# Expert loop started before the last shared sum, result rows released by the next down product, expert numbers loaded in fours, first batch's statistics at the loop's end

## The chip, the cores and the metric
One core of one Trainium2 chip runs the whole program. The metric is device time in microseconds (us) of one execution; less is better. The kernel before took 603.58 us (median of 3 runs, 598.58 to 605.2).

## The reference
Tokens are 2 batches of 1024, 128 wide, float32. Three blocks run in a row, each adding to or replacing the activations:

1. a recurrent mixing block (RWKV-like, 16 heads), its output projected,
2. a feed-forward block with 32 experts (used twice: after block 1 and after block 3),
3. a hierarchical block attention over 5 levels, 16 heads of 64.

The feed-forward block is what the change is about. In short:

```
x_n   = layernorm(x)
probs = x_n @ gate_w ; e = argmax ; score = sigmoid(max)      # one expert per token
routed = (silu(r @ gate_e) * (r @ up_e)) @ down_e,  r = x_n * score
shared = (silu(x_n @ sg) * (x_n @ su)) @ sd
x      = x + shared + routed
```

The attention block begins with a layernorm of x and a projection to queries, keys and values for 8 pairs of heads and 2 batches.

## The kernel before, in words
The program is written by hand: each engine (TensorE, VectorE, ScalarE, GpSimd, SyncE) has its own instruction list, and semaphores order them. There is no planner. The order of the lists is: mixing block (`a_*`), feed-forward 0 (`f_*`, k = 0), attention (`b_*`), feed-forward 1 (`f_*`, k = 1), stores.

**Routing.** Every token is written with its row number into a DRAM table `sorted_x` that is sorted by expert, in slots of 32 rows; every expert's part is filled up to whole slots. Four slots (128 rows, usually of four experts) are one run, and there are 24 runs. The slots of batch 0 come first.

**Shared part.** It goes by chunks of 512 tokens (4 of them, `STEPS`): `shared_in` (line 1138), a silu on ScalarE, a product on VectorE (`product_shared`, line 1159), `shared_out` (line 1144), and `add_shared` (line 1166), which adds bank 6 into `x_tok`. `keep_clock` and `keep_busy` are matmuls whose result is not used.

**Expert loop.** Per run s the engines do:

- SyncE: `fetch` (line 1441) brings 128 rows from `sorted_x`; `weights` (line 1436) brings the weights of the fourth slot's expert from DRAM (384 KB).
- TensorE (lines 1250 to 1260), in this order: `find(s)` loads the first slot's expert number into a register; `turn_in(s+1)` (1221) transposes the rows of the next run; `gate_up(s)` (1230) makes 4 products 32 rows high, each with another expert's weights; `down(s-2)` (1246); `turn_h(s-1)` (1237).
- ScalarE (lines 1307 to 1315): `copy_in` (1286), `copy_weights` (1301, second slot's weights within SBUF), `gate` (1291, silu), `copy_y` (1296).
- VectorE (lines 1374 to 1380): `copy_h` (1363), `product` (1357), `copy_weights` (1368, third slot's weights).
- GpSimd (lines 1421 to 1427): `address` (1417) casts the row numbers; an indirect DMA (1426) writes the result rows of the run to `y_tok` in token order, released by `copy_y`.

Each `value_load` brings one number with a check of its bounds. `down(s)` needs `copy_h(s)`, `copy_h(s)` needs `turn_h(s)`, and `turn_h(s)` needs `product(s)`.

**After the loop.** SyncE waits for all 24 indirect writes, then reads `y_tok` back in four chunks of 256 KB (1461). VectorE adds each chunk to `x_tok` (`add_experts`, 1386). For k = 0 VectorE then makes the means and variances (1900 to 1906), GpSimd the power -1/2 (`norm_power`, 175), VectorE the normalised rows (1911), TensorE turns them (1601), ScalarE copies them (1803), and the first attention projections start (1635). For k = 1 the four chunks are stored (2195).

```
for s in range(-1, RUNS + 2):
    if 0 <= s < RUNS:
        find(s)
    if s + 1 < RUNS:
        turn_in(s + 1)
    if 0 <= s < RUNS:
        gate_up(s)
    if 0 <= s - 2:
        down(s - 2)
    if 0 <= s - 1 < RUNS:
        turn_h(s - 1)
```

## Time and profile before

| what | value |
|---|---|
| runs | 598.58, 603.58, 605.2 us |
| profiled execution | 601.5 us, of which the span of the instructions is 599.7 us |
| mean granted TensorE clock | 0.970 |
| TensorE busy | 535.7 us (89%) |
| VectorE, ScalarE, GpSimd busy | 426.2, 288.4, 268.4 us |
| chain that ended last | TensorE 66%, VectorE 20%, issue 6%, DMA 3% |
| first expert loop | from about 168 to 225 us |
| second expert loop | from about 529 to 587 us |

The span is the time from the first to the last instruction of the profiled execution; 1.8 us lie around it. Busy shares are of the whole span and say little about one stage; the chain of waits and the timeline of a stage do.

### The profile page before, as it was taken

How to read it: one execution, taken by the hardware profiler on the slowest of the kernel's cores; microseconds unless marked ns; L12 is line 12 of the kernel's file. 1: busy time of each engine (PE TensorE's matmuls, PEld its weight loads, DVE VectorE, ACT ScalarE, POOL GpSimd, SP SyncE). 2: the span in 40 equal slices, each digit the busy share in tenths (PEclk: the TensorE clock that was granted, in tenths of full speed). 3: DMA queues.
4: the chain of work that ended last, by engine and by line, in shares of the span. 5: the costliest groups of instructions: out<-in, count | busy, mean ns of one | idle time of the engine just before them, and what ended most of it. 6: DMA issues, size and time to landing. Idle time of an engine off the chain costs nothing.

```text
span 599.7 us, 17096 instructions
## 1 busy us (share of the span) xinstructions
PE 535.7 (89%) x6454; PEld 312.7 (52%) x6454; DVE 426.2 (71%) x931; ACT 288.4 (48%) x624; POOL 268.4 (45%) x342
## 2 busy tenths in 40 slices
PE   6989978879889988999999999999999769889980
PEld 3323323445443333577767777777766646443430
DVE  3396699988245644888889888998789887345552
ACT  4633443454256641656645554456554234166750
POOL 2467666735316562333335443343222345416651
PEclk9999899998999999999999999999999787999996
DMA  5898800001728843000000000000000001628855
GB/s 170 357 429 163 107 0 2 0 0 42 215 77 222 229 129 120 14 15 20 20 22 20 20 21 20 20 20 20 20 20 7 8 2 35 206 65 226 232 142 155
DMA packets 45329, 54.14 MB, mean 90 GB/s; under 512 B 10880, under 2 KB 36416, under 8 KB 44224
## 3 DMA queue, kind: packets, MB, share of 16 engines
q1 hardware_dynamic: 42688, 47.78, 28.3%
q0 software_dynamic: 2560, 5.26, 2.5%
q8 instruction: 53, 0.87, 0.6%
q14 instruction: 28, 0.23, 0.1%
HBM read 43.55 MB, written 9.48 MB: 88 GB/s over the span
## 4 chain that ended last, share of the span: by engine, by line
PE 66%; DVE 20%; issue 6%; DMA 3%; ACT 2%; POOL 1%; another core or an unknown queue 0%; SPq 0%; DVEq 0%; POOLq 0%; ACTq 0%
PE psum L1230 8%; PE psum L1653 7%; PE psum L1635 7%; PE psum L1726 5%; PE psum L1246 4%; PE psum L1705 4%; PE psum L1141 3%; PE psum L1237 3%; PE psum L1150 3%; PE psum L1674 3%; DVE arena L757 2%; PE psum L274 2%; PE psum L1179 2%; DVE arena L751 2%; PE psum L275 2%
## 5 line engine op out<-in xcount | busy, mean ns | idle before, releaser
L2114 POOL TENSOR_TENSOR arena<-arena 128x512 f32<-128x512 f32 x32 | 40.5, 1287 | 113.3 <-issue 104.3
L1426 POOL DMA_INDIRECT y_tok<-arena,to x48 | 55.0, 1145 | 61.2 <-ACT arena L1296 54.5
L1820 ACT ACTIVATE arena<-psum 128x512 f32<-128x512 f32 x64 | 38.1, 597 | 47.3 <-PE psum L1635 44.3
L1635 PE MATMUL psum<-arena 128*128 128x512 f32 x128 | 59.2, 605 | 0.7 <-ACT arena L1803 0.7
L1230 PE MATMUL psum<-experts,arena 128*32 x96 | 50.0, 603 | 1.8 <-issue 1.2
L1230 PE MATMUL psum<-arena 128*32 128x512 f32 x288 | 50.9, 605 | 0.0
L657 POOL TENSOR_TENSOR arena<-arena 128x512 f32<-128x512 f32 x32 | 37.2, 1180 | 27.9 <-DVE arena L757 17.5
L1363 DVE COPY arena<-psum 128x256 f32<-128x256 f32 x48 | 20.4, 425 | 40.6 <-PE psum L1237 40.6
L1653 PE MATMUL psum<-arena 128*128 128x128 f32 x384 | 47.5, 278 | 0.8 <-ACT arena L1825 0.8
L1301 ACT ACTIVATE arena<-experts 128x768 f32 x48 | 40.3, 844 | 14.5 <-issue 14.4
L1653 PEld LDWEIGHTS psum<-arena 128*128 128x128 f32 x384 | 45.2, 192 | 1.8 <-ACT arena L1825 1.8
L2051 POOL TENSOR_TENSOR arena<-arena 128x256 f32<-128x256 f32 (+4 forms) x75 | 33.7, 449 | 26.2 <-ACT arena L1839 19.2
L1635 PEld LDWEIGHTS psum<-arena 128*128 128x128 f32 x128 | 22.9, 189 | 35.4 <-issue 33.8
L1395 POOL DMA_INDIRECT sorted_x<-arena,row x32 | 31.1, 973 | 19.8 <-DVE row L1091 11.3
L1246 PEld LDWEIGHTS psum<-experts,arena 128*32 128x32 f32 x192 | 18.0, 109 | 40.7 <-issue 40.4
L757 DVE TENSOR_TENSOR_SCAN arena<-psum,arena 128x512 f32<-128x512 f32 x32 | 39.1, 1266 | 0.0
L1705 PE MATMUL psum<-arena 64*64 64x64 f32 (+2 forms) x1728 | 37.4, 226 | 1.7 <-ACT arena L1835 0.9
L1965 DVE TENSOR_TENSOR x_tok<-x_tok,psum 128x512 f32<-128x512 f32 x30 | 20.6, 687 | 23.0 <-PE psum L1726 23.0
L1828 ACT ACTIVATE arena<-psum 128x512 f32<-128x512 f32 x48 | 28.7, 598 | 17.2 <-PE psum L1653 17.2
L1705 PEld LDWEIGHTS psum<-arena 64*64 64x64 f32 x1728 | 33.5, 139 | 5.9 <-ACT arena L1839 1.3
L1726 PE MATMUL psum<-arena 128*128 128x128 f32 x256 | 34.0, 286 | 2.7 <-POOL arena L2114 2.7
L751 DVE TENSOR_TENSOR arena<-arena,psum 128x512 f32<-128x512 f32 x32 | 19.9, 684 | 20.9 <-PE psum L290 20.7
(240 smaller groups left out, 1220.0 us busy)
## 6 DMA issues: line engine op xcount, KB each, us to landing
arena<-in_experts SPq DMA_DIRECT2D x48, 384.0 KB
experts<-in_experts SPq DMA_DIRECT2D x8, 1536.0 KB, 17.3
arena<-sorted_x SPq DMA_DIRECT2D x48, 64.5 KB
sorted_x<-zeros SPq DMA_DIRECT2D x2, 1536.0 KB, 13.0
arena<-in_w_qkv SPq DMA_DIRECT2D x16, 192.0 KB, 2.6
arena<-y_tok SPq DMA_DIRECT2D x8, 256.0 KB, 3.7
x_tok<-in_x SPq DMA_DIRECT2D x4, 256.0 KB, 3.8
arena<-in_w_out SPq DMA_DIRECT2D x16, 64.0 KB, 1.9
```

The source lines that it names most:

```text
L657: pool.tensor_tensor(a_g[m % HALF], a_r[c % 2], a_state[:, m, 0:CHUNK], ALU.mult).then_inc(s["g"], 1)
L757: dve.tensor_tensor_scan(a_state[:, m, 1:CHUNK + 1], DECAYS[:, :], a_kv[m % HALF], a_state[:, m, 0:1], ALU.mult, ALU.add).then_inc(s["stat ...
L1230: mm = pe.matmul(bank[2 + s % 2][rows, :], f_gxt[s % 2][:, rows], weights, start=True, stop=True)
L1246: mm = pe.matmul(bank[6 + s % 2][SLOT_ROWS * j:SLOT_ROWS * j + SLOT_ROWS, 0:C], f_sht[s % 2][:, rows], weights, start=(half == 0), stop=(h ...
L1301: act.activation(f_w_act[s % 5], experts[:, bass.ds(at, WROW)], ACT.Copy).then_inc(t["w_act"], 1)
L1426: pool.indirect_dma_start(out=y_tok, out_offset=bass.IndirectOffsetOnAxis(ap=f_to[:, s:s + 1], axis=0), in_=f_gy[s % 4], in_offset=None).t ...
L1635: pe.matmul(ring("in", n, j)[:, :], b_w[n % 2][:, which * P:which * P + P], x, start=True, stop=True)\
L1653: mm = pe.matmul(ring("in", n, 5 + i // 4)[:, i % 4 * P:i % 4 * P + P], x, b_w[n % 2][:, 2 * P:3 * P], start=True, stop=True)
L1705: mm = pe.matmul(place(Y[r][out]), b_v[n % 2][rows, i, out], e[rows, head, i - part.start, cols], start=(i == 0), stop=last_place(r, i, cols))
L1726: mm = pe.matmul(ring("out", n, i // 4)[:, i % 4 * C:i % 4 * C + C], b_yn[:, i * P:i * P + P], b_wo[n % 2], start=(n < LAST - 1 or n < LAS ...
L1820: act.activation((b_q, b_k)[which][:, part * CHUNK:part * CHUNK + CHUNK], src, ACT.Copy, scale=(D_B ** -0.5, 1.0)[which]).then_inc(h["drai ...
L2114: pool.tensor_tensor(b_yn[:, part], b_y[:, part], b_rec[:, part], ALU.mult).then_inc(h["normed"], 1)
```

## The change
1. TensorE turns the rows of run 0 before the last `shared_out`, and waits for the last `add_shared` only ahead of `down(0)`. VectorE copies the weights of runs 0 to 2 before its last `add_shared` and stays three runs ahead. `find` follows `turn_in`.
2. TensorE, ScalarE and VectorE load four expert numbers at a time, without the check of bounds, from a table laid out by slot of the run. Waits of TensorE that others imply are left out (`w_act`, `w_dve`, `y_copied`).
3. `address` goes from GpSimd to VectorE. The indirect write of run s waits for `down(s+1)` as well.
4. SyncE reads chunks 0 and 1 back as soon as 16 runs have been written. For k = 0 chunk 0 is added, measured and its power made within the loop; for k = 1 chunks 0 and 1 are added there and stored early.
5. Attention: 4 idle matmuls in place of 12, and 1 left out; buffers are laid out anew so that the early ones do not overlap the loop's; `attention_weights_in` is issued before the last read back; `add_bias(0)` follows `merge(0)` on GpSimd.

```diff
+FIRST_RUNS = (TOK // BATCH // SLOT_ROWS + EXPERTS) * SLOT_ROWS // P
+FOUND = 4
 # TensorE
                 shared_in(pe, k, c)
                 keep_clock(2)
+                if c == STEPS - 1:
+                    turn_in(0)
                 shared_out(pe, k, c)
             done(pe, "placed", 2)
-            done(pe, "down", STEPS)
             def find(s):
-                expert_at[s] = pe.value_load(f_slot_at[0:1, SIDE * s:SIDE * s + 1], min_val=0, max_val=(EXPERTS - 1) * WROW)
+                _, values = nc.values_load_multi_w_load_instructions(
+                    f_slot_at[0:1, s:s + FOUND], [pe.engine], min_val=0, max_val=(EXPERTS - 1) * WROW,
+                    skip_runtime_bounds_check_because=SLOT_BOUND)
+                expert_at.update(zip(range(s, s + FOUND), values))
             def gate_up(s):
                 done(pe, "gxt", s + 1)
-                done(pe, "w_act", s + 1)
-                done(pe, "w_dve", s + 1)
+                if s < 2:
+                    done(pe, "w_act", s + 1)
+                if s < 3:
+                    done(pe, "w_dve", s + 1)
             def down(s):
                 done(pe, "sht", s + 1)
-                done(pe, "y_copied", s - 1)
+                if s == 0:
+                    done(pe, "down", STEPS)
+                if s >= RUNS - 2:
+                    done(pe, "y_copied", s - 1)
             for s in range(-1, RUNS + 2):
-                if 0 <= s < RUNS:
+                if 0 <= s < RUNS - 1:
+                    turn_in(s + 1)
+                if 0 <= s < RUNS and s % FOUND == 0:
                     find(s)
-                if s + 1 < RUNS:
-                    turn_in(s + 1)
 # VectorE
+            for c in range(late, STEPS):
+                if c == STEPS - 1:
+                    done(dve, "rows", 1)
+                    dve.wait_ge(loaded_experts, 16 * EXPERT_LOADS)
+                    for s in range(3):
+                        copy_weights(s)
+                add_shared(dve, k, c)
+                if c + 1 < STEPS:
+                    product_shared(dve, k, c + 1)
+
             for s in range(0, RUNS + 1):
                 if s >= 1:
                     copy_h(s - 1)
                 if s < RUNS:
                     product(s)
-                if s + 2 < RUNS:
-                    copy_weights(s + 2)
+                if s + 3 < RUNS:
+                    copy_weights(s + 3)
+                if s < RUNS:
+                    address(s)
+                if k == 0 and s == RUNS - 2:
+                    chain(add_experts(dve, k, 0))
+                if k == 0 and s == RUNS - 1:
+                    measure_x(dve, chain, 0)
+                if k == 1 and RUNS - 2 <= s < RUNS:
+                    add_experts(dve, k, s - RUNS + 2).then_inc(final, 1)
 # GpSimd
-            for s in range(2):
-                address(s)
             for s in range(RUNS):
-                if s + 2 < RUNS:
-                    address(s + 2)
                 done(pool, "to", s + 1)
                 done(pool, "y_copied", s + 1)
+                if s + 1 < RUNS:
+                    done(pool, "y", s + 2)
                 pool.indirect_dma_start(out=y_tok, ...).then_inc(returned[s % 4], 16)
+                if k == 0 and s == RUNS - 3:
+                    norm_power(pool, LN_B, b_stats[0][:, 1:2 * CT:2], b_rstd[0])
 # SyncE, after the loop's fetch and weights
+            read_back(range(0, EARLY), FIRST_RUNS)
+            if k == 0:
+                for n in range(2):
+                    attention_weights_in(sp, n)
+            else:
+                for c in range(EARLY):
+                    store(sp, c)
+            read_back(range(EARLY, STEPS), RUNS)
 # attention, TensorE, VectorE, GpSimd
-            keep_busy(12)
+            keep_busy(4)
+            front_done(pe, 0, "y_copied", RUNS)
             turn_x(0)
-            keep_busy(1)
-            statistics(0)
             statistics(1)
-            norm_x(0)
+            normalise_x(dve, 0)
+            normalise_x(dve, 1)
-            power(0)
             power(1)
             pack(0)
-            add_bias(0)
...
                     merge(0)
+                    pool.wait_ge(h["merged"], MERGES)
+                    add_bias(0)
```

## Rows read from the trace of the kernel before

**Rows 1.** Windows: busy of PE, PEld, DVE, ACT, POOL, then clock, DMA share, GB/s.
```profile
548.00:560.00 12.00, 11.73 (x155) 4.85 (x151) 7.05 (x17) 8.27 (x21) 7.18 (x11) 1.00 0.85 245
```

**Rows 2.** Timeline of PE, start of the first loop: start, us, engine, line, tiles.
```profile
165.06 1.95 PE L1150 MATMUL psum<-shared_down,arena 128*128 128x128 f32 x16
167.84 0.30 PE L1221 MATMUL psum<-const,arena 128*128 128x128 f32 x1 [0.83 <-issue]
...
169.08 0.61 PE L1230 MATMUL psum<-experts,arena 128*32 x1
```

**Rows 3.** Timeline of PE, first loop: the turns of runs 3, 4, 5 and 23.
```profile
172.00 0.32 PE L1221 MATMUL psum<-const,arena 128*128 128x128 f32 x1 [0.21 <-issue]
...
174.21 0.27 PE L1221 MATMUL psum<-const,arena 128*128 128x128 f32 x1
...
176.12 0.27 PE L1221 MATMUL psum<-const,arena 128*128 128x128 f32 x1
...
217.06 0.32 PE L1221 MATMUL psum<-const,arena 128*128 128x128 f32 x1
```

**Rows 4.** Line 1213 (value_load on PE's sequencer): ns min/median/max, first and last start.
```profile
L1213 PEldq TENSOR_LOAD <-slot_at x48: 299/303/488, 167.9 to 580.1; - x48
...
L1213 PEldq SEQ_ASSERT  x48: 18/18/32, 168.7 to 580.7; - x48
```

**Rows 5.** Timeline, run 0's down and copy (first loop), then one step of the second.
```profile
173.38 0.27 PE L1246 MATMUL psum<-experts,arena 128*32 x1
...
174.06 0.28 ACT L1296 ACTIVATE arena<-psum 128x128 f32<-128x128 f32 x1
...
543.27 0.29 PE L1246 MATMUL psum<-experts,arena 128*32 x1
...
543.70 1.25 POOL L1426 DMA_INDIRECT y_tok<-arena,to  x1 [0.94 <-ACT arena L1296]
...
545.09 0.42 DVE L1363 COPY arena<-psum 128x256 f32<-128x256 f32 x1 [1.00 <-PE psum L1237]
...
545.66 0.29 PE L1246 MATMUL psum<-experts,arena 128*32 x1
```

**Rows 6.** Timeline from the first loop's last release to the first projection.
```profile
226.31 0.96 POOL L1426 DMA_INDIRECT y_tok<-arena,to  x1 [0.67 <-issue]
...
232.01 0.69 DVE L1386 TENSOR_TENSOR x_tok<-x_tok,arena 128x512 f32<-128x512 f32 x1 [7.88 <-DMA arena<-y_tok]
...
232.74 0.87 DVE L1900 BATCH_NORM_STATS2 arena<-x_tok 128x6 f32<-128x128 f32 x4
...
234.32 1.41 POOL L175 TENSOR_TENSOR arena<-arena,const 128x4 f32<-128x4 f32 x1 [7.05 <-DVE arena L1906]
...
236.26 1.11 DVE L1911 TENSOR_SCALAR arena<-x_tok,arena 128x128 f32<-128x128 f32 x4
...
237.42 0.65 PE L1601 MATMUL psum<-const,arena 128*128 128x128 f32 x4 [2.01 <-DVE arena L1911]
...
240.12 3.70 PE L1635 MATMUL psum<-arena 128*128 128x512 f32 x8 [0.69 <-ACT arena L1803]
```

**Rows 7.** Timeline, end of the program.
```profile
586.73 0.28 ACT L1296 ACTIVATE arena<-psum 128x128 f32<-128x128 f32 x1 [1.34 <-PE psum L1246]
587.77 0.96 POOL L1426 DMA_INDIRECT y_tok<-arena,to  x1 [0.67 <-issue]
...
593.05 1.51 DVE L1386 TENSOR_TENSOR x_tok<-x_tok,arena 128x512 f32<-128x512 f32 x2 [7.46 <-DMA arena<-y_tok]
...
595.15 1.46 DVE L1386 TENSOR_TENSOR x_tok<-x_tok,arena 128x512 f32<-128x512 f32 x2 [0.59 <-DMA arena<-y_tok]
```

**Rows 8.** Timeline, first coarsen operation on DVE, in attention's first step.
```profile
242.77 1.87 DVE L1983 TENSOR_TENSOR arena<-arena 128x128 f32<-128x128 f32 x1 [0.97 <-ACT arena L1820]
```

**Rows 9.** Line 1368, VectorE's weight copies: ns min/median/max, first and last start.
```profile
L1368 DVE COPY arena<-experts x48: 559/561/697, 168.1 to 580.1; 128x768 f32 x48
```

**Rows 10.** Timeline, shared_out of the second feed-forward at a lower granted clock.
```profile
498.16 3.76 PE L1150 MATMUL psum<-shared_down,arena 128*128 128x128 f32 x16
```

More of the change, by code:

```diff
@@ L49 @@
 RUNS = SLOTS * SLOT_ROWS // P
+FIRST_RUNS = (TOK // BATCH // SLOT_ROWS + EXPERTS) * SLOT_ROWS // P
+FOUND = 4
+SLOT_BOUND = "second_places keeps the expert of a slot between 0 and EXPERTS - 1"
 ROW = C + 1
@@ L891, in hybrid_block @@
         f_to = sb("to", [P, RUNS], U32)
+        F_LOOP_AT = used[0]
         f_gx = [carve(ROW) for _ in range(8)]
@@ L1347, in f_dve @@
             chain(dve.tensor_scalar(f_slot_row[0:1, :], bank[7][0:1, 0:SLOTS], float(WROW), None, ALU.mult))
-            dve.tensor_copy(f_slot_at[0:1, :], f_slot_row[0:1, :]).then_inc(t["rows"], 1)
-            for c in range(late, STEPS):
-                add_shared(dve, k, c)
-                if c + 1 < STEPS:
-                    product_shared(dve, k, c + 1)
+            dve.tensor_copy(f_slot_at[0:1, :].rearrange("o (j s) -> o s j", j=SIDE), f_slot_row[0:1, :].rearrange("o (s j) -> o s j", j=SIDE)).then_inc(t["rows"], 1)
             def product(s):
@@ L1453, in f_sp, with read_back @@
                 fetch(s)
+            def read_back(chunks, steps):
+                for j in range(4):
+                    sp.wait_ge(returned[j], 16 * (RUNS // 4 * k + steps // 4))
+                for c in chunks:
+                    sp.dma_start(tiles_of(f_back[:, c * CHUNK:c * CHUNK + CHUNK]),
+                                 y_tok[c * CHUNK:c * CHUNK + CHUNK].rearrange("(i p) c -> p i c", p=P)).then_inc(gathered[c], 16)
             for s in range(6, RUNS):
@@ L1872, in b_act @@
                     front_score(act, 1, 0)
+                if n == 0:
+                    for j in range(4):
+                        act.wait_ge(returned[j], 16 * (RUNS // 4))
                 if now:
@@ L1898, in statistics @@
                 chain(add_experts(dve, 0, c))
[L1899 to L1913 removed]
+                measure_x(dve, chain, c)
             def shift(c):
@@ L2192, in _ @@
             f_sp(sp, 1)
-            for c in range(STEPS):
-                sp.wait_ge(final, c + 1)
-                sp.dma_start(out[c * CT:c * CT + CT].rearrange("i p c -> p i c"),
-                             tiles_of(x_tok[:, c * CHUNK:c * CHUNK + CHUNK])).then_inc(stored, 16)
+            for c in range(EARLY, STEPS):
+                store(sp, c)
             sp.wait_ge(stored, 16 * STEPS)
@@ L2227, in _ @@
             f_dve(dve, chain, 1)
-            for c in range(STEPS):
+            for c in range(EARLY, STEPS):
                 add_experts(dve, 1, c).then_inc(final, 1)
```

105 lines of the change are left out of this document (59 added, 46 removed).

## The prediction

> **What bounds the kernel now.** I read the chain of waits first: it is TensorE for two thirds and passes through both expert loops, so the loops and the gaps behind them are on the path. Then I read the timeline of four places. (a) In the loops the turns of runs 3 and 23 start at 172.00 and 217.06, so 20 steps take 45.06 us, 2.25 us each; between runs 4 and 5 one takes 1.91 us [rows 3]. That shortest step is what TensorE's own instructions need. The difference, 0.34 us, is what the loop can give at most. (b) Ahead of the loop TensorE ends the last shared_out at 165.06 + 1.95 = 167.01, stands for 0.83 us until the last shared sum is in x_tok, turns run 0 at 167.84 and starts gate_up(0) at 169.08 [rows 2]. (c) Behind the first loop nothing useful runs on TensorE between its last down, which ends near 225, and the first projection at 240.12 [rows 6]. (d) Behind the second loop the path is release, read back of four chunks, add, store [rows 7].
>
> **Why a step takes 2.25.** Two things compete. The first is the lookup of the expert number: TensorE's sequencer is held from the start of the load to the end of the assert, 0.6 us (580.1 to 580.7), 0.8 at worst [rows 4], every step, between turn_h and turn_in. The second is longer. In run 0, before any result is released, ScalarE can read down's result 0.68 us after down starts (173.38 to 174.06). In the second loop down starts at 543.27, a release on GpSimd at 543.70, and VectorE's copy_h, ready for 1.00 us, starts only at 545.09, or 1.82 after down; the next down follows at 545.66 [rows 5]. So the step was 2.39 us, and it went round down, late signal, copy_h (0.42), down. My reading is that TensorE's signals come late while GpSimd issues an indirect write: copy_h starts 545.09 - 543.70 = 1.39 after the release started. The rows show it by time alone; the cause is inferred. If x is the start of the release after the start of down, a step bound this way takes x + 1.39 + 0.42 + 0.15 = x + 1.96, and x is 0.43 here.
>
> **The change, part by part.**
>
> *Start of the loops.* After it, turn_in(0) lies before shared_out (+0.3 us of TensorE), turn_in(1) follows, and gate_up(0) no longer waits for the shared sum. Expert numbers are loaded while shared_out's matmuls are queued. gate_up(0) starts at 167.01 + 0.3 + 0.2 = 167.5, not 169.08: 1.6 us less [rows 2]. Run 0's silu no longer sits behind a late weight copy, worth another 0.3. I take 1.9 per loop, 3.8 in all. VectorE's three weight copies and their load (about 0.6 + 3 x 0.56, an estimate) fit between its last product and the shared sum, whose adding hides them; if they did not, gate_up(1) would wait, and the gain is 1.0 per loop. Bounds 2.0 to 4.4.
>
> *Steps.* The lookup goes from every step to every fourth, and two waits go. The check goes, but the price of four loads in one has no row. From below it is one load, 0.30; from above four in a row, 1.2 [rows 4]. I take 0.7: most of it lies under matmuls already queued. The Trainium skill (DMA: Bandwidth & Descriptors, section Latency and other measured facts) gives such a load a floor of about 600 ns and says that the compiler unrolls by four to spread it. By that figure, an estimate, four loads in one would cost 0.6, and the sum would stay. The trace has 0.30 for one and decides.
> The release of run s now waits for down(s+1). In the trace a release starts 0.75 us behind what frees it (ScalarE's copy of the last run ends at 586.73 + 0.28 = 587.01 and the release starts at 587.77) [rows 7]. Freed by the signal of down, itself x + 1.35 late, it starts at x' = x + 1.35 + 0.75 - step, and with step = x + 1.96 this settles at x = 0.14, step = 2.10. Before, the copy in between (0.3) made it 0.43 and 2.39. So the ceiling of a slow step falls from 2.39 to 2.10, and no step is under 1.91. The mean before was 2.25, since some steps escape; I take 2.09 after. That is 0.16 x 21 steps x 2 loops = 6.7 us. Bounds: all steps 1.91, 14.3 us; no gain, 0.
> address on VectorE (about 0.1 to 0.2 per step, an estimate from its small casts) is hidden by the 1.00 us that VectorE stands before copy_h [rows 5]; it comes on the path only if that idle time is gone. On GpSimd it was hidden too.
> DMA engines are busy 0.85 at 2.3 us a step [rows 1]; at 2.09 that makes 0.94. Weights are issued some four steps ahead, so a lag of 0.05 a step is covered. I take 0.
> A rule speaks about the same place. VectorE's weight copy starts about 0.9 us after down's signal (copy_h and product come first, an estimate from their 0.42 each); the release starts 1.05 after it now (0.28 of copy, then 0.75) and 0.75 after it in future, so the two change places. The trace has 48 weight copies of 0.561 us, the longest 0.697 [rows 9], so none ever stood behind a release. The Trainium skill (SBUF — State Buffer) says that a copy of VectorE within SBUF and a GpSimd instruction take a shared port pair in turn, and that whoever is second stands still. What that would do here is rival B.
>
> *First loop's end and start of attention.* Old path: last release 226.31, chunk 0 added at 232.01, statistics, power, normalised rows, turned at 237.42, project at 240.12 [rows 6]. New path, in the old clock: measure_x(0), 0.87 + 0.38 + 0.17 = 1.5 with gaps [rows 6], stands ahead of copy_h(23) and delays the last down by 0.8, to 225.1. Its signal is 1.0 later, the release of run 22 starts 0.75 after that, at 226.8, that of run 23 at 228.1, and ends at 229.1. power(1) is queued on GpSimd behind both: about 1.2 us (1.41 in the row), to 230.3. Normalising chunk 1 takes 1.11, to 231.45, turning 0.65, copying 0.65: first projection at 232.8. Gain 240.1 - 232.8 = 7.3 us. Chunk 0 is normalised by 228.1 and does not bind; four idle matmul pairs (3.5 us) end near 229.3 and don't either. The new wait of GpSimd for down holds both releases and power(1) behind it, which is counted. Chunks 2 and 3 are read from 231 and wanted after 239. What could eat it: chunk 0's read back is issued behind the last weights; if it lands late, VectorE waits in step 22 with copy_h(22) behind. I find 1 to 2 us of room. Bounds 5 to 8.5.
>
> *Clock.* With 8 idle matmuls fewer, TensorE is busy for about a third of the 3.5 us before the projections. At the level of 1.2 GHz a shared_out took 3.76 us [rows 10] and at 2.4 GHz 1.95 [rows 2]. The projections take 3.70 [rows 6], so a fall costs 0 to 3.4 us. I take 1.0.
>
> *add_bias(0).* Beside it VectorE's first coarsen operation took 1.87 us [rows 8], and that is no longer on VectorE's way. It goes behind merge(0), where GpSimd waits for the next result anyway, but beside VectorE's softmax work. I take 0; the bounds are that one wait in either place, 1.9 lost or 1.9 won.
>
> *End.* Two chunks remain to be read, added and stored. The last add ended at 595.15 + 1.46 = 596.61; with two, adds start at 593.05 and end by 594.5 [rows 7]: 2.05 less. The release of run 22 waits for down(23) and not for its own copy, which puts the last one 0.95 later. Gain 1.1, bounds 0 to 2.
>
> **Sum.** 3.8 + 6.7 + 7.3 - 1.0 + 0 + 1.1 = 17.9 us. The profiled execution took 601.5, so 583.6 by its own time; the median of the runs shown is 603.6, 2.1 above it, which gives 585.7. I say 585.
>
> **The rivals.** Within 1% (6 us) is about what a measurement here cannot tell from no change.
> - *A: releases leave down's signal alone* (x falls outside). All steps at 1.91 to 1.95: 14 us in place of 6.7, 578. For: run 0, with no release beside it, and steps of 1.91. Against: a release is 1 us long and starts 0.75 after a signal, so in a 1.9 us step it reaches into the next down. Chance 0.2.
> - *B: the port in turn*, where a release that starts first holds VectorE's copy for its 0.96 us: the copy ends 0.75 + 0.96 + 0.56 = 2.27 after the signal, copy_h follows, steps of 2.4: 0.15 x 42 = 6.3 us lost, not 6.7 won, 598. For: a release is 1.25 us long beside VectorE's copy and 0.96 alone [rows 5, 7]. Against: no copy was longer than 0.70 us [rows 9], though in the trace releases and copies overlap in many steps. Chance 0.1.
> - *C: slower.* The four loads come as a burst on TensorE, ScalarE and VectorE, 1.25 us each, at three different steps of four. If nothing hides them, a step costs 1.91 + 3 x 1.25 / 4 = 2.85, 0.6 more than now: +25 us against 11 won elsewhere, 617. It decides from about 2.5 us a step. For: ScalarE is busy 8.27 us of 12 [rows 1] and must fit its own. Against: such a lookup is made on each of them in every step today. Chance 0.04.
> - *D: the shadow.* The attention phase is bound by something that does not move earlier, so the 7.3 are given back there: 592. For: chunks 2 and 3 and the second batch come by the same SyncE list. Against: they are asked for 8 us ahead, and TensorE is busy nearly throughout that phase in the page's slices. Chance 0.08.
> - The forecast: 0.58.
>
> **How the numbers follow.** The forecast's own range is 579 to 592. A reaches to 574, B to 599. I take 574 to 597, which leaves C, most of B and the extremes out. Faster by over 1% (below 597.5): all of forecast and A, most of D, a third of B: 0.86. Within 1%: 0.10. Slower: 0.04.
>
> **What would show it.** The mean distance of turns in both loops near 2.09, with copy_h about 1.4 us after a release starts. gate_up(0) about 0.5 us after the last shared_out, with no idle time for the shared sum. First projection 8 us or less after the last down ends, against 15. Two adds at the end. I am wrong if steps stay at 2.25, if ScalarE or VectorE shows one long gap in every fourth step, if VectorE waits for chunk 0 in step 22, or if the clock falls between the loop and attention.

## The result, and the profile after

The changed kernel took 585.22 us (median of 4 runs, 581.5 to 588.44) beside 601.38 for the kernel before (598.58 to 605.2): a ratio of 0.972, 95% interval 0.967 to 0.978. The prediction was 585 us with a range of 574 to 597. The profiled execution took 581.5 us, its span 579.7. The time came out; what stands behind one term of the sum did not, and the experiments are mostly about that.

The page after says:

| what | before | after |
|---|---|---|
| span | 599.7 us | 579.7 us |
| TensorE, VectorE, ScalarE, GpSimd busy | 535.7, 426.2, 288.4, 268.4 us | 521.2, 425.8, 286.8, 250.3 us |
| mean granted clock | 0.970 | 0.971 |
| chain: TensorE, issue, VectorE, DMA | 66, 6, 20, 3% | 54, 18, 15, 8% |

The busy columns hardly move. What moved is read from the timeline. First the turns of runs 3 and 23 (PE; start, us, engine, line, operation), for [rows 3]:

```profile
167.89 0.27 PE L1187 MATMUL psum<-const,arena 128*128 128x128 f32 x1
...
210.09 0.27 PE L1187 MATMUL psum<-const,arena 128*128 128x128 f32 x1
```

20 steps take 42.20 us, 2.11 each, where they took 2.25. The start of the first loop, for [rows 2], again PE alone:

```profile
160.95 1.88 PE L1183 MATMUL psum<-shared_up,const 128*128 128x512 f32 x4
...
163.20 0.33 PE L1187 MATMUL psum<-const,arena 128*128 128x128 f32 x1 [0.36 <-DMA arena<-sorted_x]
...
163.36 1.96 PE L1154 MATMUL psum<-shared_down,arena 128*128 128x128 f32 x16
...
165.36 0.62 PE L1240 MATMUL psum<-experts,arena 128*32 x1
```

`gate_up(0)` follows the last `shared_out` at once (163.36 + 1.96 = 165.32, then 165.36), where 2.07 us lay between them. But the turn of run 0 now stands ahead of `shared_out`, and waited 0.36 us for its rows. The lookup, for [rows 4], and VectorE's weight copies, for [rows 9] (ns min/median/max, first and last start), then the window for [rows 1]:

```profile
L1222 PEldq TENSOR_LOAD <-slot_at x12: 327/332/519, 163.6 to 554.0; - x12
```

```profile
L1398 DVE COPY arena<-experts x48: 553/628/633, 162.0 to 558.2; 128x768 f32 x48
```

```profile
548.00:560.00 12.00, 11.38 (x146) 4.70 (x146) 7.19 (x23) 7.97 (x23) 5.19 (x6) 1.00 0.82 238
```

Four numbers cost 0.33 us, one cost 0.30. The copies went from 0.56 to 0.63 us (medians). One steady step of the first loop, for [rows 5]:

```profile
196.24 0.29 PE L1259 MATMUL psum<-experts,arena 128*32 x1
...
196.38 0.96 POOL L1481 DMA_INDIRECT y_tok<-arena,to  x1 [1.23 <-ACT arena L1309]
...
197.81 0.28 ACT L1309 ACTIVATE arena<-psum 128x128 f32<-128x128 f32 x1 [0.73 <-PE psum L1259]
197.86 0.42 DVE L1380 COPY arena<-psum 128x256 f32<-128x256 f32 x1 [0.82 <-PE psum L1247]
...
198.42 0.29 PE L1259 MATMUL psum<-experts,arena 128*32 x1
```

The write starts 0.14 us after `down`, `copy_h` 1.48 us after the write, and the next `down` 2.18 after the last one. Behind the first loop, for [rows 6] (last `down`, filling products, the powers and releases on GpSimd, norm, projection):

```profile
217.84 0.29 PE L1259 MATMUL psum<-experts,arena 128*32 x1 [1.10 <-DVE arena L1380]
...
218.68 5.09 PE L1687 MATMUL psum<-const 128*128 128x512 f32 x8
...
219.16 1.05 POOL L178 TENSOR_TENSOR arena<-arena,const 128x4 f32<-128x4 f32 x1
...
220.41 1.09 POOL L1481 DMA_INDIRECT y_tok<-arena,to  x1 [0.20 <-issue]
...
221.81 0.96 POOL L1481 DMA_INDIRECT y_tok<-arena,to  x1 [0.30 <-issue]
222.79 1.04 POOL L178 TENSOR_TENSOR arena<-arena,const 128x4 f32<-128x4 f32 x1
...
223.87 1.11 DVE L1445 TENSOR_SCALAR arena<-x_tok,arena 128x128 f32<-128x128 f32 x4 [2.35 <-POOL arena L178]
...
226.38 3.70 PE L1716 MATMUL psum<-arena 128*128 128x512 f32 x8 [0.69 <-ACT arena L1884]
...
229.03 0.29 DVE L2053 TENSOR_TENSOR arena<-arena 128x128 f32<-128x128 f32 x1 [0.97 <-ACT arena L1901]
```

The chain runs through GpSimd's queue: two releases, then power(1), then the norm of chunk 1. From last `down` to projection it takes 8.54 us, where it took 15.85. The eight filling products take 5.09 us because the granted clock was 0.50 from 219 to 221 us; it was 1.00 again from 222 us on, ahead of the projection. The last row answers to [rows 8]: the first coarsen operation takes 0.29 us, not 1.87. And the end, for [rows 7] (last release, then the add of the last two chunks, where [rows 7] has two such adds):

```profile
570.02 0.96 POOL L1481 DMA_INDIRECT y_tok<-arena,to  x1 [0.30 <-issue]
...
575.35 1.39 DVE L1430 TENSOR_TENSOR x_tok<-x_tok,arena 128x512 f32<-128x512 f32 x2 [8.91 <-DMA arena<-y_tok]
```

### The profile page after: what moved, and what is told of

It is laid out like the page before. It is cut to its first block, busy times and chain, and to the rows that moved or that the text cites. A ratio compares the mean times of both kernels' runs of the same rounds, so it can differ in the third digit from the quotient of the medians.

```text
span 579.7 us, 16589 instructions
## 1 busy us (share of the span) xinstructions
PE 521.2 (90%) x6436; PEld 308.9 (53%) x6436; DVE 425.8 (73%) x979; ACT 286.8 (49%) x624; POOL 250.3 (43%) x294
## 4 chain that ended last, share of the span: by engine, by line
PE 54%; issue 18%; DVE 15%; DMA 8%; ACT 2%; SPq 1%; POOL 1%; POOLq 0%; ACTq 0%; DVEq 0%
PE psum L1240 8%; PE psum L1734 7%; PE psum L1716 7%; DMA sorted_x<-zeros 5%; PE psum L1807 5%; PE psum L1259 5%; PE psum L1786 5%; PE psum L1247 3%; PE psum L1755 3%; PE psum L1796 1%; DVE arena L2056 1%; PE psum L1154 1%; DVE arena L2053 1%; DVE arena L2015 1%; DVE arena L760 1%
## 5 line engine op out<-in xcount | busy, mean ns | idle before, releaser
L1481 POOL DMA_INDIRECT y_tok<-arena,to x48 | 46.5, 968 | 85.9 <-ACT arena L1309 85.1
L1240 PE MATMUL psum<-experts,arena 128*32 x96 | 50.2, 604 | 2.7 <-ACT arena L1299 1.1
L1240 PE MATMUL psum<-arena 128*32 128x512 f32 x288 | 50.9, 605 | 0.0
L1380 DVE COPY arena<-psum 128x256 f32<-128x256 f32 x48 | 20.4, 425 | 36.7 <-PE psum L1247 35.9
L1456 POOL DMA_INDIRECT sorted_x<-arena,row x32 | 31.2, 976 | 20.4 <-DVE row L1095 11.8
L1909 ACT ACTIVATE arena<-psum 128x512 f32<-128x512 f32 x48 | 28.7, 599 | 17.2 <-PE psum L1734 17.2
L1259 PE MATMUL psum<-experts,arena 128*32 x192 | 30.2, 280 | 5.1 <-DVE arena L1380 4.3
```

The source lines that it names most:

```text
L1240: mm = pe.matmul(bank[2 + s % 2][rows, :], f_gxt[s % 2][:, rows], weights, start=True, stop=True)
L1259: mm = pe.matmul(bank[6 + s % 2][SLOT_ROWS * j:SLOT_ROWS * j + SLOT_ROWS, 0:C], f_sht[s % 2][:, rows], weights, start=(half == 0), stop=(h ...
L1481: pool.indirect_dma_start(out=y_tok, out_offset=bass.IndirectOffsetOnAxis(ap=f_to[:, s:s + 1], axis=0), in_=f_gy[s % 4], in_offset=None).t ...
```

## The experiments

Twelve runs were made in four groups, each group beside its own runs of the kernel before. That kernel took 583.6 and 583.1 us in groups 1 and 4, and 600.7 and 601.1 in groups 2 and 3. The chip had number 2 in groups 1 and 2, number 9 in group 3 and 14 in group 4, so its number does not tell the two levels apart; what does is not known. Only ratios and profiles within one level are compared. I call them level 601 and level 583. The profiles, cut at the first and last `down` of each loop, in us:

| kernel | to first down | loop 1 | to projection | to 2nd first down | loop 2 | to end |
|---|---|---|---|---|---|---|
| before, two profiles (601) | 173.4, 169.1 | 50.9, 51.4 | 15.9, 15.9 | 294.5, 294.2 | 51.1, 50.4 | 14.0, 13.8 |
| changed, two profiles (601) | 169.0, 170.2 | 48.9, 48.8 | 8.5, 8.5 | 291.6, 291.6 | 48.6, 49.4 | 13.1, 13.1 |
| no early start (601) | 169.2 | 48.7 | 8.5 | 294.7 | 48.5 | 13.2 |
| no early sums (601) | 170.4 | 48.7 | 17.2 | 293.3 | 48.9 | 13.1 |
| no down wait (601) | 170.8 | 49.7 | 6.8 | 290.7 | 48.9 | 11.8 |
| address wait (601) | 172.3 | 45.4 | 7.5 | 293.2 | 45.9 | 12.0 |
| no down wait (583) | 166.8 | 43.9 | 7.6 | 290.0 | 43.4 | 11.4 |
| address wait (583) | 168.1 | 44.4 | 7.5 | 289.5 | 43.3 | 11.6 |

A loop here is 23 steps, from its first `down` to its last. The two profiles of one kernel differ by up to 0.7 us in a loop, so a smaller difference between kernels tells nothing.

### Group 1 (level 583): what sets the step?

**e1_no_down_wait.** The releases no longer wait for the next down product.

```diff
-                if s + 1 < RUNS:
-                    done(pool, "y", s + 2)
```

> The changed kernel without the wait of the releases for the down product of the run after theirs; everything else as changed. Theory (TensorE's signals reach the other engines late while GpSimd issues an indirect write, so where the write starts within a step sets the step): the write of run s starts as soon as the copy of its result is out, as in the kernel before, some 0.43 us after the start of a down product, the copy of h begins about 1.4 us after that, and a step is 0.43 + 1.96 = 2.4 us in the steady stretches, about 2.3 over 20 turns, against 2.11 now. Two loops of about 22 steps: 8 to 11 us slower than the changed kernel, near 594 us. Rival 1 (the lookups made the steps shorter, the wait only lets DVE run): steps stay at 2.1 and the time within 1 us of the changed kernel. Rival 2 (the wait itself costs, since it delays the releases to the loop's end): steps stay and the tail is shorter, 1 to 2 us faster.

Measured 566.29 us, ratio 0.971 (0.966 to 0.975), and nearly every step is 1.91 us.

**e2_plain_write.** The results are written to rows in order, so that placing them by token is left out.

```diff
-                pool.indirect_dma_start(out=y_tok, out_offset=bass.IndirectOffsetOnAxis(ap=f_to[:, s:s + 1], axis=0),
-                                        in_=f_gy[s % 4], in_offset=None).then_inc(returned[s % 4], 16)
+                pool.dma_start(y_tok[(s // 16 * 8 + s % 8) * P:(s // 16 * 8 + s % 8) * P + P, :], f_gy[s % 4]).then_inc(returned[s % 4], 16)
```

> The changed kernel in which GpSimd starts a plain write of the same 128 rows of 512 bytes at the same place of its program instead of the indirect one; the results go to the wrong tokens' rows, so the placing of the results by token is left out. Theory (late signals come from GpSimd's building of the indirect write): a plain write takes GpSimd less time, so the copy of h is no longer held until 1.4 us after the write's start, and steps fall from 2.11 to 1.9 to 1.95 us, as in the steps of the changed kernel where no write falls on the signal: 44 steps by 0.16 to 0.2, 7 to 9 us faster, near 577 us. Rival 1 (the step of 2.1 is set by TensorE, DVE or the weights' transfers and the write is only beside it): steps stay at 2.1, time within 1.5 us. Rival 2 (any write that GpSimd starts itself holds the signals, plain or indirect): steps stay at 2.1 or shift with the write's start, with the copy of h still 1.4 us behind it.

Measured 566.49 us, ratio 0.970 (0.965 to 0.975), steps of 1.91; the write keeps GpSimd for 0.54 us in place of 0.99. With indirect writes beside it at the same 1.91, this tells nothing of the cause.

**e3_address_wait.**

```diff
-                if s + 1 < RUNS:
-                    done(pool, "y", s + 2)
+                if s + 2 < RUNS:
+                    done(pool, "to", s + 3)
```

> The changed kernel in which the release of run s waits for DVE's address of run s + 2 in place of TensorE's down product of run s + 1: the release starts about 0.4 us earlier in the step, some 0.3 us ahead of the start of a down product instead of 0.14 us behind it, and its start no longer hangs on a signal of TensorE. Theory (signals held until 1.4 us after the write's start): the hold is over at about 1.1 us in the step, before the turn of h is done, so the copy of h is not delayed: steps of 1.91 to 1.95 us instead of 2.11, 44 steps, 7 to 9 us faster than the changed kernel, near 577 us. Rival 1 (the wait's place is indifferent, the step is bound by something else): steps stay at 2.1. Rival 2 (the hold now falls on the signal of the gate products, so ScalarE's gate is late and its weight copy with it): steps get longer than 2.15 and the time rises by 2 us or more.

Measured 567.41 us, ratio 0.973 (0.969 to 0.977), steps of 1.91.

**e4_single_loads.** On TensorE, and so on ScalarE and VectorE:

```diff
-                _, values = nc.values_load_multi_w_load_instructions(
-                    f_slot_at[0:1, s:s + FOUND], [pe.engine], ...)
-                expert_at.update(zip(range(s, s + FOUND), values))
+                expert_at[s] = pe.value_load(f_slot_at[0:1, s:s + 1], min_val=0, max_val=(EXPERTS - 1) * WROW)
```

> The changed kernel with the lookups as before, one number at a time with its bounds check, on TensorE, ScalarE and DVE; releases and all else as changed. Theory (TensorE is not what bounds a step at 2.1 us, the copy of h is, and the lookup lies beside it): what is lost is at most the difference of a checked load to the quarter of a four-number load on DVE's way from its weight copy to the copy of h; DVE has 0.3 us or more left there, so steps stay at 2.11 to 2.2 us and the time rises by 0 to 4 us, taken 2. Rival (the lookups were what made the steps 2.25 and the wait did nothing): steps return to 2.2 to 2.3 and the time rises by 6 us or more.

Measured 567.44 us, ratio 0.973 (0.969 to 0.977), most steps 1.91. From the start of the last `shared_out` to the first `down` it takes 6.25 and 6.06 us in the two loops, 5.60 with loads in fours: the lookups in fours are worth about 0.5 us at each start and nothing in a step of 1.91.

All four went against the reading of the profile after: steps of 1.91 with the wait, without it, with a plain write. The rows say why. e1 has a write that starts 0.04 us after `down`, as the changed kernel has once. ScalarE's copy (L1309) needs `down`'s signal, `copy_h` (L1380) that of `turn_h`. First the changed kernel:

```profile
176.63 0.27 PE L1259 MATMUL psum<-experts,arena 128*32 x1
...
176.67 0.96 POOL L1481 DMA_INDIRECT y_tok<-arena,to  x1 [1.21 <-ACT arena L1309]
...
178.12 0.28 ACT L1309 ACTIVATE arena<-psum 128x128 f32<-128x128 f32 x1 [0.47 <-PE psum L1259]
178.16 0.42 DVE L1380 COPY arena<-psum 128x256 f32<-128x256 f32 x1 [0.84 <-PE psum L1247]
```

Then e1:

```profile
176.34 0.27 PE L1259 MATMUL psum<-experts,arena 128*32 x1
...
176.38 1.13 POOL L1479 DMA_INDIRECT y_tok<-arena,to  x1 [1.19 <-ACT arena L1309]
...
177.03 0.28 ACT L1309 ACTIVATE arena<-psum 128x128 f32<-128x128 f32 x1
...
177.37 0.42 DVE L1380 COPY arena<-psum 128x256 f32<-128x256 f32 x1 [0.63 <-PE psum L1247]
```

The same places of the same work: the copy of `down`'s result starts 1.49 us after `down` in one and 0.69 in the other. In the profiles of group 1 the late signals are not there. So group 1 tested neither theory, and both kernels had to be profiled in one group.

### Group 2 (level 601): the starts and the sums

**e5_before_again**, **e6_after_again.** Both kernels unchanged.

> The kernel before, unchanged, once more with a profile, on the chip of this group of runs. In the first four experiments every step took 1.91 us, whatever the releases waited for, and TensorE's signal of a down product came 0.66 us after its start with an indirect write running beside it; the kernel before took 583.6 us there and not 601. Theory 1 (the chip of those runs does not show the late signals at all, the one of the first two profiles does): on such a chip the kernel before has steps near 1.91 to 1.95 us too, its time is near 584, and the changed kernel's gain is made of the starts, the attention's start and the end alone, 13 to 16 us. Theory 2 (late signals are there for the kernel before alone, from GpSimd's own address copies or its checked lookups): steps near 2.2 us and a gain that includes 10 us or more of steps. On a chip of the first kind: 600 us and steps of 2.25.

> The changed kernel, unchanged, on the same chip as the kernel before with a profile. Theory 1: if the kernel before is near 584, steps of 1.91 us and a time near 567, like the four experiments, ratio 0.972; of the 16 us some 5 lie at the two loops' starts, 7 at the attention's start, 1 at the end, 0 to 2 in the steps. If the kernel before is near 600: steps of 2.11 and 585. Theory 2: steps of 1.91 here against 2.2 of the kernel before.

The kernel before took 596.7 us in its one profiled run here (median of its seven other runs 600.7), the changed one 584.74, ratio 0.973 (0.966 to 0.981). Steps are 2.27 and 2.14 us again (the second to the twentieth step of each loop, mean of both loops, stalls included). This group was of the other level, so what the kernel before does at level 583 was not profiled. That its 17 us there come from steps without late signals is an inference: the kernel without the down wait is 14.7 us quicker at level 583 than at 601, and 11.3 of these lie in the two loops.

**e7_no_early_start.**

```diff
                 keep_clock(2)
-                if c == STEPS - 1:
-                    turn_in(0)
                 shared_out(pe, k, c)
 ...
             done(pe, "placed", 2)
+            done(pe, "down", STEPS)
+            turn_in(0)
```

VectorE's first three weight copies go back behind its last shared sum.

> The changed kernel with the start of the loops as before: the first turn after the last shared sum, TensorE's wait for the shared product's copies ahead of the loop, and VectorE's first three weight copies after its shared sums. Theory (the start was 2.7 us shorter per loop by the two profiles): 4 to 5.5 us slower than the changed kernel, 2 to 2.7 at each loop's first down product. Rival (the start is bound by the scattered rows' and weights' transfers, which come when they come): within 1 us of the changed kernel.

Measured 584.47 us, ratio 0.972 (0.965 to 0.979): by the medians no difference from the changed kernel. The four runs of each, side by side in this group, took 583.35 to 585.99 us and 583.46 to 586.41, so the 4 to 5.5 us of the theory are not there, and the rival's number (within 1 us) came true. Its reason did not, for the profile has the stretch itself longer. From the last filling products (L1183) to the first `down`, PE of e7:

```profile
160.09 1.88 PE L1183 MATMUL psum<-shared_up,const 128*128 128x512 f32 x4
...
161.81 1.95 PE L1154 MATMUL psum<-shared_down,arena 128*128 128x128 f32 x16
...
164.58 0.43 PE L1187 MATMUL psum<-const,arena 128*128 128x128 f32 x2 [0.83 <-DVE x_tok L1173]
...
165.62 0.61 PE L1240 MATMUL psum<-experts,arena 128*32 x1 [0.61 <-ACT arena L1299]
...
169.23 0.27 PE L1259 MATMUL psum<-experts,arena 128*32 x1
```

9.14 us (8.99 in the second loop), against 8.02 and 7.43 in the changed kernel and 10.03 and 9.83 before. So the earlier order gives 1.1 us at the first loop, where the turn waited for its rows ahead of `shared_out`, and 1.6 at the second. The other 0.9 us between e7 and the kernel before comes with the lookups in fours (0.5, e4) and the rest. Where the 2.7 us of the two stretches went in the whole time is not shown. The runs of e7 had granted clocks of 0.968 to 0.976, those of the changed kernel 0.965 to 0.971, and e7's profile has no long stall in its loops; either can hide a part.

**e8_no_early_sums.**

```diff
-            read_back(range(0, EARLY), FIRST_RUNS)
+            read_back(range(0, EARLY), RUNS if k == 0 else FIRST_RUNS)
 # VectorE and GpSimd: chunk 0's sum, statistics and power
-                if k == 0 and s == RUNS - 2:
-                    chain(add_experts(dve, k, 0))
 ...
-                if k == 0 and s == RUNS - 3:
-                    norm_power(pool, LN_B, b_stats[0][:, 1:2 * CT:2], b_rstd[0])
 ...
+            statistics(0)
             statistics(1)
```

> The changed kernel with the first chunk of the first loop read back after all releases, and its sum, statistics and power after the loop, as before; the second loop is as changed. Theory (the first projection comes 7.3 us sooner after the last down product because this work is already done by then): 5 to 8 us slower than the changed kernel, all of it between the first loop's last down product and the first projection. Rival (the shorter stretch comes from the bias sum moved away from GpSimd and the fewer filling products): under 2 us slower.

Measured 592.26 us, ratio 0.984 (0.977 to 0.991): 7.5 us slower than the changed kernel of the same group, and 8.7 in the stretch itself. VectorE stands for the transfer after the releases again, as in [rows 6]:

```profile
227.82 0.69 DVE L1426 TENSOR_TENSOR x_tok<-x_tok,arena 128x512 f32<-128x512 f32 x1 [8.89 <-DMA arena<-y_tok]
...
236.28 5.45 PE L1710 MATMUL psum<-arena 128*128 128x512 f32 x8 [0.69 <-ACT arena L1878]
```

This is not the early sums alone. e8 keeps the 4 idle matmuls of the change where the kernel before had 12, so TensorE stood idle from 225.0 to 233.3 us, the granted clock was 0.50 from 231 to 238, and the first projections took 5.45 us in place of 3.70. Some 1.75 us of e8's loss are this clock. A version with late sums and all 12 idle matmuls was not run. In the change the sums are early, and the fewer idle matmuls cost nothing on the path; with late sums they do.

### Group 3 (level 601): the wait again

**e9_no_down_wait_2**, the kernel of e1.

> The changed kernel without the releases' wait for the down product, once more: in the first group no step showed a late signal, and the kernel before took 584 us there; in the second group it took 601 us, the late signals were there (steps of 2.27 us before, 2.13 changed). If the kernel before is near 601 in this group, theory (the write's start in the step sets the step): steps of 2.25 to 2.38 us instead of 2.13, 5 to 11 us slower than the changed kernel's 585 of its group, 590 to 596 us. Rival (lookups or VectorE's order made the difference of 0.14 us, the wait none): steps of 2.13, 585 us. If the kernel before is near 584: steps of 1.91 and 566 us again, and neither is tested.

Measured 580.97 us, ratio 0.967 (0.965 to 0.970). Both expectations miss: steps are 2.18 us (mean of 19), between the wait's 2.14 and the 2.27 of the kernel before, and the time is lower, not higher, than with the wait. The steps do follow the write's start. Two in a row:

```profile
178.95 1.17 POOL L1479 DMA_INDIRECT y_tok<-arena,to  x1 [0.58 <-issue]
...
179.21 0.29 PE L1259 MATMUL psum<-experts,arena 128*32 x1 [0.20 <-DVE arena L1380]
...
180.41 0.42 DVE L1380 COPY arena<-psum 128x256 f32<-128x256 f32 x1 [0.34 <-PE psum L1247]
...
181.15 0.27 PE L1259 MATMUL psum<-experts,arena 128*32 x1
...
181.39 1.06 POOL L1479 DMA_INDIRECT y_tok<-arena,to  x1 [1.27 <-ACT arena L1309]
```

A write 0.26 us ahead of `down` gives a step of 1.94; the next, 0.24 behind it, one of 2.22; one 0.42 behind, 2.31 to 2.36. The three alternate.

This trace also shows a part of what the other edits do. In e9 a write 0.1 us or more ahead of `down` goes with a step of 1.96 us (mean of 11), in the kernel before with one of 2.12 (mean of 16 in two profiles, 12 of them between 2.10 and 2.29). The turn and `gate_up` that follow the `down` at 179.21 in e9:

```profile
180.06 0.27 PE L1187 MATMUL psum<-const,arena 128*128 128x128 f32 x1
...
180.27 0.62 PE L1240 MATMUL psum<-experts,arena 128*32 x1
```

Then a step of the kernel before, its write 0.22 us ahead of `down`, and the load of its lookup (ns min/median/max, first and last start):

```profile
200.47 0.29 PE L1246 MATMUL psum<-experts,arena 128*32 x1
...
201.41 0.33 PE L1221 MATMUL psum<-const,arena 128*128 128x128 f32 x1
...
201.74 0.61 PE L1230 MATMUL psum<-experts,arena 128*32 x1
...
202.62 0.27 PE L1246 MATMUL psum<-experts,arena 128*32 x1
```

```profile
L1213 PEldq TENSOR_LOAD <-slot_at x1: 309/309/309, 200.7 to 200.7; - x1
```

The load starts at 200.7, its assert at 201.3, and the turn only then, 0.94 us after `down` and not 0.85; `gate_up` starts at 1.27 and not 1.06, and the step is 2.15 and not 1.94. So in steps that no late signal holds, the lookup does, together with the waits that were left out behind it. By the two means (0.16 us on 11 of 38 steps, an estimate) that is about half of the 0.09 us between 2.27 and 2.18.

What the wait costs is in the table: the last releases and what is queued behind them come 1.8 us later ahead of attention and 1.3 at the end.

**e10_address_wait_2**, the kernel of e3.

> The changed kernel with the releases waiting for VectorE's address of run s + 2, once more, for the same reason. If the kernel before is near 601 in this group, theory (a write started 0.3 us ahead of a down product holds TensorE's signals only until about 1.1 us in the step, ahead of the signal that the copy of h needs): steps of 1.91 to 1.95 instead of 2.13, 7 to 9 us faster than the changed kernel, 576 to 579 us. Rival (the held gate signal makes ScalarE late): steps of 2.15 or more, 585 us or more. If the kernel before is near 584: steps of 1.91 and 567 us again.

Measured 575.21 us, ratio 0.956 (0.955 to 0.958). This is the version that beats both kernels: 26 us under the kernel before, and 10 under the changed one by ratios whose intervals lie apart. At level 583 it gave nothing over the kernel without any wait (e3 567.41 us, e1 566.29). One step:

```profile
181.37 0.96 POOL L1481 DMA_INDIRECT y_tok<-arena,to  x1 [1.20 <-ACT arena L1309]
...
181.86 0.27 PE L1259 MATMUL psum<-experts,arena 128*32 x1
...
182.90 0.42 DVE L1380 COPY arena<-psum 128x256 f32<-128x256 f32 x1 [0.64 <-PE psum L1247]
```

The write starts 0.49 us ahead of `down` (0.73 in every other step). `copy_h` is free at 182.90, its result is out before `gate_up` ends, and the next `down` starts at 183.77, after 1.91 us. The same trace has the opposite case late in the loop, where VectorE has no weight copy left and its address comes sooner:

```profile
211.03 0.27 PE L1259 MATMUL psum<-experts,arena 128*32 x1
...
211.75 0.96 POOL L1481 DMA_INDIRECT y_tok<-arena,to  x1 [0.49 <-issue]
...
213.17 0.42 DVE L1380 COPY arena<-psum 128x256 f32<-128x256 f32 x1 [2.21 <-PE psum L1247]
...
213.74 0.29 PE L1259 MATMUL psum<-experts,arena 128*32 x1 [0.26 <-DVE arena L1380]
```

A write 0.72 us behind `down`, `copy_h` 1.42 after the write, and a step of 2.70. One kernel, one loop, two places of the write, 1.91 and 2.70. VectorE's work differs between the two steps as well, but e3 is the same kernel at level 583: there the same step has its write 0.78 us behind `down`, `copy_h` starts 1.03 after `down`, and the step takes 2.08. So at level 601 the place of the write sets the step, by way of the late signal.

### Group 4 (level 583): what is left

**e11_address_back.** The releases wait for their copies alone, and the address goes back to GpSimd.

```diff
             for s in range(RUNS):
+                if s + 2 < RUNS:
+                    address(s + 2)
                 done(pool, "to", s + 1)
                 done(pool, "y_copied", s + 1)
-                if s + 1 < RUNS:
-                    done(pool, "y", s + 2)
```

> The changed kernel without the releases' wait for the down product and with the address copies back on GpSimd, as in the kernel before; the lookups stay in fours. Where the kernel before is near 601: steps were 2.27 us before, 2.18 with the wait alone taken out of the changed kernel, 2.13 in it. Theory (the address on GpSimd makes each release longer, 1.25 us of GpSimd's time in place of 1.06, and its start later): steps of 2.25 to 2.29 us, 3 to 4.5 us slower than the 581 of the kernel without the wait, 584 to 586. Rival (the lookups in fours bring the step from 2.27 to 2.18): steps of 2.17 to 2.19, within 1 us of 581. Where the kernel before is near 584: steps of 1.91 and nothing told.

Measured 566.09 us, ratio 0.970 (0.967 to 0.973); steps of 1.91. It fell on level 583, so it does not tell which edit took the step from 2.27 to 2.18; what is known of that stands at e9.

**e12_address_wait_19.**

```diff
-                if s + 2 < RUNS:
+                if s + 5 < RUNS:
                     done(pool, "to", s + 3)
```

> The changed kernel with the wait for VectorE's address of run s + 2 on the releases 0 to 18 alone; the last five releases wait for nothing but their copies. In the version with that wait on all, steps were 1.91 but for the third last of each loop, 2.70 and 2.89 us, where VectorE has no weight copy left, its address comes 0.6 us sooner and the write starts 0.71 us into the step. Theory: without the wait there, that step falls to 2.3 or less and the loops' tails are some 0.3 to 0.7 us shorter: 1 to 2 us faster than the 575.2 us of that version, if the kernel before is near 601; 564 to 566 if it is near 584. Rival (the last releases now start together at a worse place): the same or up to 1 us slower.

Measured 565.96 us, ratio 0.971 (0.968 to 0.974), against 0.973 (0.969 to 0.977) for e3: no difference that can be told at this level. The case it was made for, 2.70 us at level 601, was not tested.

## Why the prediction came out, point by point

- **Start of the loops**, taken as 1.9 each, 3.8 in all. Measured from the last filling products to the first `down`: 10.03 to 8.02 and 9.83 to 7.43, 4.4 in all. Right for the stretch, with a part I had not priced: the turn of run 0 waits for a transfer ahead of `shared_out` (0.36 us in the row). That it is worth this much in the whole time is not shown: e7 took 2.7 us of it back and was no slower.
- **Steps**, taken as 2.25 to 2.09 and 6.7 us. The turns give 2.11 in loop 1. The loops are shorter by 2.3 and 1.8 us (means of two profiles each), 4.1 in all. The shape of the steady step was right: write 0.14 us behind `down`, step x + 1.96 = 2.10 against 2.1 to 2.2 in the rows. **The step that failed is the cause of the gain.** I gave all of it to the new wait, by the reasoning that the ceiling of a slow step falls from 2.39 to 2.10. With the wait taken out (e9) the step is 2.18, so some two thirds of the 0.13 us between 2.27 and 2.14 come with the other edits. I had named the lookup as the first of two things that compete, and then priced its going at nothing; the rows at e9 show it in the way. What the wait wins, 0.7 us by whole loops (one profile, and within the spread of two profiles of one kernel) or 1.7 by the mean steps, is less than the 3.1 us that it costs behind the two loops. Without it the kernel is 3 us faster by the ratios, 0.967 against 0.972 and 0.973, but the intervals overlap (0.965 to 0.970 against 0.967 to 0.978), so this is likely and not shown. That no step is under 1.91 was wrong at the loop's end, where nothing is left to turn: the last one took 1.63.
- **Stalls**, taken as 0 on the ground that the weights are ordered some four steps ahead. They are ordered mostly 4.7 to 5.6 us ahead of their `gate_up`, two and a half steps, where it was 5.5 to 6.2 before. Each loop has one or more stalls, up to 1.4 us long, and both profiles of the kernel before have none over 0.5. In the first loop `gate_up(10)` waits 1.11 us at 185.31, and its weights were issued at 178.95; in the second a `gate_up` waits 0.76 us at 540.44, by the profile for the DMA from `in_experts`. So what failed here is the cover of the weights' transfer. Why a transfer is late is not shown. DMA engines are no busier than before, 0.82 to 0.86, where I had worked out 0.94. The stalls cost less than their length: behind one, the write lies ahead of `down`, and the next three steps take 1.92, 1.91 and 1.91 us in place of 2.15.
- **Attention's start**, taken as 7.3. Measured 15.85 to 8.54, 7.3; e8 undoes it and costs 7.5. The path was the one named: two releases, power(1), norm, turn. I had counted the last `down` 0.8 us later within it and the stretch down to 7.7. The last step is in fact 0.5 longer (2.12 for 1.63), which the table counts in the loop, and the stretch is 8.5, since the power of chunk 0 stands right ahead of the release of run 22 on GpSimd (219.16 to 220.21). So the term as I had it is some 6.8. It is the largest and the one the runs show best, though 1.75 us of what e8 loses are the clock.
- **Clock**, taken as 1.0 lost. My sign of being wrong did come: between loop and attention the granted clock fell to 0.50 in both profiles of the changed kernel (219 to 221 us, and 220 to 223 in e6), and in none of the kernel before, of e9 or of e10. TensorE had waited 1.06 and 1.10 us ahead of its last two `down`. But it was back before the projections, which take 3.70 us as before, and the filling products that ran at it are not on the path. Nothing was lost there; e8 shows what is lost when it does not come back.
- **add_bias(0)**, taken as 0. The coarsen operation is 1.58 us shorter, yet attention's phase, less what its end gains at the second start (2.4), is only 0.4 us shorter, no more than two profiles of one kernel differ by.
- **End**, taken as 1.1. Measured 0.8 (13.9 to 13.1). Without the down wait it would have been 2.1, near the 2.05 that the two missing adds gave in my working.
- **The rivals.** A's steps of 1.91 come when the write lies ahead of `down`, which the change's wait does not do and the address wait does. B, the port in turn: the copies beside a write are 0.63 us for 0.56, not a whole release longer, and 0.80 at most in e10, where the copy starts 0.5 us into the write. By that rule of the Trainium skill (SBUF — State Buffer) the step would have been 2.4, and the trace disagrees. C: a load of four is 0.33 us, not 1.25, and no gap comes with every fourth step; the floor of about 600 ns in the Trainium skill (DMA: Bandwidth & Descriptors, Latency and other measured facts) is not what the trace has for a load alone (0.30); only a whole lookup, from load to assert, takes 0.6. D: attention gave nothing back.

That the total hit is partly luck. The steps came 2.6 us short and the stalls were not counted, while the clock and the starts came 1.6 us better. And two misses cancelled: the gain was 16.2 us by the medians and not 17.9, and I took it from 603.6, where the kernel before then measured 601.4.

Open: how the 0.09 us from 2.27 to 2.18 divide between the lookups in fours, the waits left out and the address on VectorE; why the weights are late at times; what the earlier start is worth in the whole time; what the kernel before does in its steps at level 583; and by what means the late signals come.

## What to carry to other kernels

When a loop's period depends on where a side job lands in it, ask what starts that job, and move its trigger, not its work: at level 601 the wait for VectorE's address in place of TensorE's product took most steps from 2.15 to 1.91 us with the same instructions. Beware of a trigger that the job itself delays: with both such triggers tried here, `down` and its copy, the loop stayed slow (2.14 and 2.18). When a loop's step is held by two things, price both, also the one that is shorter: it holds the steps that escape the other. Take idle matmuls out only together with the wait that they fill: left without them, e8 lost clock. And price a new wait also by its last turn: behind the loop it held two releases and what was queued behind them, 3.1 us, more than it had won.

## What the runs showed of the hardware

- At level 601, where an indirect write of GpSimd starts between 0.32 us ahead of `down` and 0.74 behind it, `copy_h`, which waits for TensorE, starts 1.3 to 1.6 us after the write in all but 4 of 238 such cases (eight profiles, the second to the twentieth step of each loop). At level 583 this does not happen: in e1 `down`'s result is read 0.69 us after its start with a write beside it. The same kernel differs by 3% between the two (581.0 and 566.3 us), at a granted clock of 0.973 and 0.970. By what means the signals are late is not shown.
- VectorE's weight copy is 0.25 us longer where it starts 0.5 us into a write (0.80 for 0.55 us, e10). Where the copy starts first, by 0.16 us, the write takes 1.25 us for 0.96 (kernel before).
- With TensorE idle from 225.0 to 233.3 us the granted clock was 0.50 from 231 to 238, and eight products of 128x512 took 5.45 us for 3.70 (e8).
- A load of four numbers takes 0.33 us, of one 0.30; a whole checked lookup of one, to its assert, 0.6.
- A plain write issued by GpSimd keeps it 0.54 to 0.60 us (e2), an indirect one 0.95 to 1.36.
